# Plain gathers for the whole first fill, two sets of transposes moved to round 12, and row indices for the joint table

## What is computed

```python
V = emb_v[x]                                   # 32 fields x 2048 x 64
iu, ju = np.triu_indices(F, k=1)               # 496 pairs
VV = V[iu] * V[ju]
hid = jax.nn.relu(jnp.einsum('pbk,kh->pbh', VV, at_w) + at_b)
score = jnp.einsum('pbh,ho->pbo', hid, at_h)
pooled = jnp.sum(VV * score, axis=0)
logit = pooled @ p + w0 + jnp.sum(w1[x], axis=0)
prob = jax.nn.sigmoid(logit)
```

## Time and profile before

| | |
|---|---|
| median of 3 runs | 843.81 us (842.17 to 844.33) |
| the profiled execution | 845.1 us, its span 843.2 us |
| PE (TensorE matmul) busy | 784.8 us, 93% |
| DVE (VectorE) busy | 721.6 us, 86% |
| ACT (ScalarE) busy | 640.4 us, 76% |
| POOL (GpSimd) busy | 538.4 us, 64% |
| share of DMA engines taken by the gathers' queue | 45.3% |
| granted TensorE clock, mean | 0.98 |

### The profile page before, as it was taken

One profiled execution on the slowest core, in us unless ns is written; L12 is line 12 of the kernel. 1 busy time (PEld: TensorE's weight loads), 2 busy tenths in 40 slices (PEclk: granted clock), 3 DMA queues, 4 the chain that ended last, 5 costly groups with the idle time before them and its releaser, 6 DMA issues.

```text
span 843.2 us, 26432 instructions
## 1 busy us (share of the span) xinstructions
PE 784.8 (93%) x10550; PEld 278.6 (33%) x10550; DVE 721.6 (86%) x1221; ACT 640.4 (76%) x676; POOL 538.4 (64%) x529
## 2 busy tenths in 40 slices
PE   0467699999999999999999999999999999999998
PEld 0123233333333333333333333333333333333332
DVE  2456678999999999999999999999999999999894
ACT  0255477888888888888888888888888888888785
POOL 4377566667767666677676666776766667767600
PEclk9869799999999999999999999999999999999999
DMA  8589625444334446543243456833445546633300
GB/s 190 157 25 25 25 21 24 21 22 24 21 21 24 22 21 22 22 24 22 20 24 23 21 22 22 24 22 20 23 22 22 22 22 23 23 21 23 12 0 2
DMA packets 19135, 24.17 MB, mean 29 GB/s; under 512 B 9704, under 2 KB 9773, under 8 KB 19117
## 3 DMA queue, kind: packets, MB, share of 16 engines
q0 software_dynamic: 16640, 17.07, 45.3%
q1 hardware_dynamic: 1535, 6.64, 2.1%
q10 hardware_dynamic: 942, 0.22, 0.1%
HBM read 20.59 MB, written 3.31 MB: 28 GB/s over the span
## 4 chain that ended last, share of the span: by engine, by line
PE 88%; POOL 4%; DMA 4%; issue 2%; ACTq 1%; DVE 0%; SPq 0%; ACT 0%; POOLq 0%
PE Z L574 53%; PE SG L590 27%; POOL rows L287 4%; PE SG L604 4%; PE Z L538 4%; DMA rows<-table,joint_idx 2%; DMA tail_w<-in_L_rec_w_dram 1%; DMA table<-tail 1%; DVE joined L344 0%; PE Z L666 0%; ACTq L476 0%; ACTq L477 0%; ACTq L478 0%; ACTq L473 0%; PE Z L647 0%
## 5 line engine op out<-in xcount | busy, mean ns | idle before, releaser
L287 POOL DMA_INDIRECT rows<-table,joint_idx x504 | 521.5, 1035 | 251.4 <-issue 146.5
L431 DVE TENSOR_TENSOR X<-V 128x992 f32<-128x992 f32 (+15 forms) x1024 | 634.8, 691 | 31.8 <-ACT V L487 18.4
L513 ACT ACTIVATE H<-Z,bias 128x1024 f32<-128x1024 f32 x512 | 528.9, 1120 | 114.3 <-PE Z L574 110.8
L574 PE MATMUL Z<-X,w_sb 64*64 64x512 f32 x4096 | 478.0, 602 | 6.8 <-DVE X L431 3.2
L574 PEld LDWEIGHTS Z<-X,w_sb 64*64 64x64 f32 x4096 | 147.3, 133 | 288.9 <-issue 282.7
L590 PE MATMUL SG<-H,score_w 128*32 128x512 f32 x2048 | 239.4, 597 | 0.0
L590 PEld LDWEIGHTS SG<-H,score_w 128*32 128x32 f32 x2048 | 56.8, 109 | 172.8 <-issue 96.2
L457 ACT ACTIVATE pV<-V,pmask 128x1024 f32<-128x1024 f32 x64 | 81.6, 1277 | 0.1
L399 DVE TENSOR_TENSOR prod<-SG,gram 128x512 f32<-128x512 f32 x32 | 22.1, 692 | 65.4 <-PE SG L590 65.4
L446 ACT COPY V<-Z 128x1024 f32<-128x1024 f32 x31 | 31.4, 1012 | 43.4 <-PE Z L538 43.4
L604 PEld LDWEIGHTS SG<-V,pV 128*32 128x32 f32 x4096 | 43.4, 110 | 21.9 <-issue 19.9
(11 more groups left out here) (46 smaller groups left out, 38.6 us busy)
## 6 DMA issues: line engine op xcount, KB each, us to landing
rows<-table,joint_idx POOLq DMA_INDIRECT x504, 3.8
table<-joined SPq DMA_DIRECT2D x4, 792.0 KB
H<-in_L_rec_emb_v_dram SPq DMA_DIRECT2D x4, 768.0 KB, 10.2
idx_raw<-in_r_x_dram SPq DMA_DIRECT2D x2, 64.0 KB, 2.0
idx_raw<-in_r_x_dram ACTq DMA_DIRECT2D x2, 64.0 KB, 2.2
rows<-in_L_rec_emb_v_dram,idx POOLq DMA_INDIRECT x8, 7.9
w_all<-in_L_rec_w_dram,idx POOLq DMA_INDIRECT x8
table<-tail SPq DMA_DIRECT2D x1, 54.7 KB
```

The source lines that it names most:

```text
L287: pool.indirect_dma_start(out=rows[t % 2][:, g * FILL_M + m, half, c0:c1], out_offset=None, in_=source, in_offset=bass.IndirectOffsetOnAxi ...
L431: last_one = nc.vector.tensor_tensor(xo, vj, vi.unsqueeze(3).to_broadcast(shape), ALU.mult)
L513: nc.scalar.activation(H[:, s % H_SLOTS, :, COLS * g:COLS * g + COLS], Z[:, z_slot(r), :, :], ACT.Relu, bias=bias[:, 0:1]).then_inc(hid_re ...
L574: done = nc.tensor.matmul(Z[64 * par:64 * par + 64, z_slot(r), half, :], w_sb[k, :], X[k, s % X_SLOTS, par, COLS * g:COLS * g + COLS], sta ...
```

## The change

Three things are changed.

1. All 16 gathers of fill 0 are plain, so only fill 1 waits for the joint table. The w1 values of fill 0 then all come from single-value gathers at the end, 16 instead of 8, and `keep_w1(0, 0)` is dropped. The counts of `w1_kept` and `w1_first` follow.
2. In fills 1 and 2 the transposes of the next fill (the third and the fourth one) stand before round 12 instead of round 6. ScalarE's `keep_v` moves with them, and its pV halves and w1 copies from relus 12 and 14 to 14 and 15. Slots and waits follow. As these two fills now differ from the rest, they are straight code on every engine, and the loop begins with fill 3.
3. A joint gather takes `table` as rows of 66 values with the row index `idx` and a constant offset of `half` values. `joint_idx` and the two VectorE operations that made it are dropped.

```diff
-TURN_BEFORE = 6
+TURN_BEFORE, LATE_TURN = 6, 12
+LATE_FILLS = (1, 2)
...
+JOINT_AT = (0, 1)
+PLAIN_FILLS = 1
...
+def turn_before(t):
+
+    return LATE_TURN if isinstance(t, int) and t in LATE_FILLS else TURN_BEFORE
...
-    return (r if r < TURN_BEFORE else r + 1) % Z_SLOTS
+    return (r if r < turn_before(t) else r + 1) % Z_SLOTS
...
-    return r - 2 if TURN_BEFORE <= r < TURN_BEFORE + 2 else r - 3
+    return r - 2 if turn_before(t) <= r < turn_before(t) + 2 else r - 3
...
             fill(0, 0, True, False)
-            with eng.Fori(1, FILLS - 2, 2) as t:
+            fill(1, 1, False, False)
+            fill(2, 0, False, False)
+            with eng.Fori(3, FILLS - 2, 2) as t:
...
-                for g in groups:
-                    joint = t > 0 or g > 0
-                    source, at_rows = (flat, joint_idx) if joint else (emb_v, idx)
+                joint = t >= PLAIN_FILLS
+                for g in range(2):
...
-                                                    in_=source,
-                                                    in_offset=bass.IndirectOffsetOnAxis(ap=at_rows[:, col:col + 1], axis=0)
+                                                    in_=table if joint else emb_v, element_offset=JOINT_AT[half] if joint else 0,
+                                                    in_offset=bass.IndirectOffsetOnAxis(ap=idx[:, col:col + 1], axis=0)
...
-            plain_w1 = [(2 * half, n) for half in range(2) for n in range(FILL_M)]
+            plain_w1 = [(Q, n) for n in range(PLAIN_FILLS * FILL_M) for Q in range(QUARTERS)]
...
-            gather(0, groups=(0,))
-            pool.wait_ge(idx_ready, 4)
+            gather(0)
+            pool.wait_ge(idx_ready, 2)
             pool.wait_ge(table_stored, 16 * (PIECES + 1))
-            gather(0, groups=(1,))
             gather(1)
             pool.wait_ge(first_turned, 2)
-            pool.wait_ge(w1_kept, 2)
             gather(2)
             for t in range(3, FILLS):
                 pool.wait_ge(rows_turned, t - 2)
-                pool.wait_ge(w1_kept, 2 * (t - 1))
+                pool.wait_ge(w1_kept, 2 * (t - 1 - PLAIN_FILLS))
                 gather(t, paced=True)
...
-            dve.wait_ge(idx_ready, 2)
-            for half in range(2):
-                cols = slice(half * 2 * NM, (half + 1) * 2 * NM)
-                nc.vector.tensor_scalar(joint_idx[:, cols], idx[:, cols], float(JOINT), float(half), ALU.mult, ALU.add
-                                        ).then_inc(idx_ready, 1)
...
-                        if r == TURN_BEFORE:
+                        late = turn_before(t) == LATE_TURN
+                        if r == turn_before(t):
                             keep_v(t + 1, 1 - parity)
-                        if r == 12:
+                        if r == (14 if late else 12):
                             keep_pv(t + 1, 1 - parity, 0)
                             keep_w1(t + 1, 1 - parity)
-                        if r == 14:
+                        if r == (15 if late else 14):
                             keep_pv(t + 1, 1 - parity, 1)
...
-                        keep_w1(0, 0)
...
-                if r == TURN_BEFORE + 2 and not first and not last:
+                if r == turn_before(t) + 2 and not first and not last:
...
-                    if r == TURN_BEFORE and not first and not last:
-                        pe.wait_ge(hid_ready, ROUNDS * t + TURN_BEFORE - Z_SLOTS + 1)
+                    if r == turn_before(t) and not first and not last:
+                        pe.wait_ge(hid_ready, ROUNDS * t + turn_before(t) - Z_SLOTS + 1)
                         turn(t + 1, 1 - parity)
...
             products(0, 0, True, False)
-            products(1, 1, False, False, head)
-            with pe.Fori(1, FILLS - 2, 2) as t:
+            products(1, 1, False, False)
+            products(2, 0, False, False)
+            products(3, 1, False, False, head)
+            with pe.Fori(3, FILLS - 2, 2) as t:
```

23 lines of the change are left out of this document (10 added, 13 removed).

## The result

| | before | after |
|---|---|---|
| median of 14 runs each | 843.55 us (842.17 to 844.90) | 847.30 us (842.40 to 850.32) |
| ratio, 95% interval | | 1.0040 (1.0026 to 1.0054) |
| the profiled execution | 845.1 us, span 843.2 | 850.3 us, span 848.0 |
| PE busy | 784.8 us | 789.7 us |

The changed kernel is 0.4% slower. The forecast was 830.4 us and a range of 822.5 to 839, so it was wrong in sign and in size. The runs of the changed kernel spread over 7.9 us, those of before over 2.7; the profiled one is its slowest, so its trace shows the loss at its largest.

What follows compares the result with a forecast made beforehand. The prediction took TensorE to bound the steady fills and a line of GpSimd and DMA gathers the head; 19.7 - 1.8 - 4.5 = 13.4 us gained, so 831.7 profiled and 830.4 us median, range 822.5 to 839.

Steps and rivals of the forecast that it cites:

- S: Delay of the joint table from eight more plain gathers beside its stores: 2.5 us taken, between 0.7 and 4.2, extreme 12.3.
- the prediction's own line: Landing time of joint gathers before the change: 34.2 us + 1.54 us x number, counted from the first one.
- Part 1: Head: eight joint gathers less before fill 1, so its transposes come at 61.4 us, ruled by landing.
- The 19.7 us at round 12: Fill 1: rounds 6 to 11 fill the wait for rows, so round 12 starts at 87.3 us instead of 107.02.
- F: Theory made after the result: TensorE's instruction blocks wait behind gathers' packets; gaps need new straight code and full DMA engines.
- The 1.8 us back in fill 3: The gap where the loop begins moves to fill 3, with no wait to lie under: 1.8 us lost.
- The late pV, 0.7 twice: Two late fills: ScalarE's pV is done 8.1 us after the transposes' start, PE wants it at 7.4; 1.4 us lost.
- Fills 3 and 4, E = 4.5 us: Fill 4's transposes wait 3.1 us for rows, fill 3's even; with 1.4 for pV, 4.5 us lost (1.4 to 8.5).
- Edits of no price: Row-wise index, eight more w1 gathers at the end and dropped fill 0 w1 copies were claimed to cost nothing.
- the rival of a longer gather: GpSimd: row-wise index with constant lengthens each joint gather; at 1.56 us, 25 us lost, giving 855; chance 0.05.
- (b): Rival at the head: table stores starved by gathers, 12.3 us late, round 12 at 97.1, giving 840.2; chance 0.12.
- (d): Rival: fetching two more straight fills while DMA engines are at 0.90 eats the 13.4 us gain, giving 843.8; chance 0.07.

Runs made afterwards that it cites:

- thin gathers: The changed kernel with every gather of fills 1 to 31 fetching one value for each partition instead of 65: 829.4 us, 0.9868 of the kernel before.
- copies: The changed kernel with gathers of fills 1 to 31 replaced by tiny transfers, plus sixty 512 KB copies on SP's queue: 852.9 us, 1.0148 of the kernel before.
- the parts alone: Kernel before with only the plain gathers and row index: 1.0141, 1.0103; with only late transposes and straight fills 1 and 2: 1.0010, 1.0013, 1.0008 of it.

## Why the prediction was wrong

**The size of S, the cost on the table.** This is the first step that failed: 2.5 us forecast, from bytes at 363 GB/s (0.7) and engine time in a light window (4.2), and 11.1 measured. The prediction's own sign of being wrong, a first joint gather after 40 us, came true at 44.19. The end called the extreme, 12.3, was the nearest. The reasoning by bytes fell: beside gathers the engines move half as much (169 to 187 GB/s). The row that said so was on hand, the first eight gathers' landing at 22.53 us beside the loads, and was put under a rival. The Trainium skill, "DMA: Bandwidth & Descriptors", section "Queues, rings and completion order", has the engines go round their queues packet by packet, and it spoke against the change. The trace agrees in so far as both queues are served in the same 15 us, the gathers' with 55.5% of the engines' time and the stores' with 39.0%; single turns it doesn't show. With 11.1 in the prediction's own line, fill 1 comes at 70.0; it came at 70.92. So eight plain gathers cost 11.1 us and save eight joint ones, 12.3: Part 1 moves work of nearly the same price from one side of the table to the other: 1.2 us by this sum, 0.3 us as measured (71.17 to 70.92). Fill 0's second group was off by the same cause: forecast between 28 and 34.8 us, it came at 38.69, which cost nothing, as fill 1's rows came later still.

**The 19.7 us at round 12.** The mechanism held: the work of rounds 6 to 11 filled the wait, no wait was left before fill 2's transposes. The gain was 10.2. Of the 9.5 us missing, 8.6 are S. In the rest is the step "that place is now straight code, so 14.5": the gap is still there with 1.48 us, in straight code. It was never the loop's entry: the row of before has it behind the 14th matmul, two ahead of the place where the loop begins. It ends 1.3 to 1.6 us after a packet of q8 in both profiles, and it is 0 with thin gathers and 2.52 with copies, so it is a wait for a block of instructions. This misreading mattered more than its size, since the gap was the one sight of F in the trace of before.

**The 1.8 us back in fill 3.** No gap of its own there; fill 3's first rounds took 1.5 us more at the lower clock, after the gaps.

**The late pV, 0.7 twice.** Fill 2's grams waited 0.44 us; fill 3's lie among the gaps, where no wait for pV can be seen. The 0.21 us at fill 1's grams isn't part of it: their order is as before, where they waited 0.83. Mechanism right, size somewhat smaller.

**Fills 3 and 4, E = 4.5 us.** No wait for rows at all: both had room. In this place stand the gaps, 9.1 us, which no term of the sum had, with some 2.5 us of matmuls at the lower clock between them, 1.5 in fill 3's first rounds, and 0.9 of short pauses in fill 4's. This is the second step that failed, and the one that turned a gain into a loss: that the filled pause costs only waits for rows, 4.5 us. The prediction saw that GpSimd's pause would go and the queue stay full, and asked only who waits for rows.

**Edits of no price.** The row index: GpSimd's mean joint gather is 1040 ns for 1035, so the rival of a longer gather is out.

```profile
L293 POOL DMA_INDIRECT rows<-table,idx x496 | 515.7, 1040 | 249.6 <-issue 144.2
```

The w1 gathers: nothing here, some 12 us on the chips of 1134 us.

**The rivals.** (b), stores starved, had round 12 9.9 us earlier, and it came 10.2 us earlier: it describes the head. From that gain it took 1.8 and 4.5 us and came to 840.2. What was lost instead in the profile after is 9.1 us of gaps, 0.4 us at the pV and some 5 us of slower or paused matmuls, 15 us, so that its span is 4.8 us longer; this execution is the slowest of 14, and the median lost 3.75 us. The gaps are (d)'s mechanism, with a chance of 0.07: fetching straight code while the engines are full. Its size was off too: not one price for each new piece of code, but a block that comes some 13 us late and the one behind it. Why this block and not those from 88 to 107 us, with the engines at 0.85 to 0.88 as well, isn't shown. The two rivals were priced as alternatives, 0.12 and 0.07, but they add. What the chances lacked is the case of both. That they are tied, because a later table and a filled pause keep the queue full when the new code is wanted, is argued and not shown.

## To carry to other kernels

A DMA that is issued earlier isn't free because the engine that issues it was idle: count what the DMA engines are doing then, and price a gather of 128 rows by the slope of its landings under load (1.54 us here; 11.1 us for eight), not by its bytes. When a pause in a long queue of gathers is filled, look for what used the pause: here TensorE's next instructions. When a gap in the middle of a row of matmuls stands at the same place in two kernels and has no releaser, look for a packet of instructions just ahead of its end. If there is one, try the unrolled code where the DMA engines have room; no run here did that with a gain.

## What the runs showed of the hardware

A block of 16 KB of TensorE's instructions came some 13 us late behind gathers, though such blocks take 0.1% of the DMA engines' time in all. Beside gathers at a share of 0.85 to 0.92 TensorE stood 5.1 and 4.0 us, and beside copies from SP's queue (1.22, with packets that overlap) 3.1 and 2.5, each time until a block had come. A full queue isn't enough by itself, as blocks also came in even steps beside a share of 0.85 to 0.88. And chips differ, or what goes on beside them: on four, the kernel before takes 1109 to 1138 us instead of 843, and on one of these the changed kernel takes 833 us without the gathers, as fast as on the others. What makes the gathers so costly there stays open; late blocks it isn't, as the loop fetches none. Open is also which part of the change brings the gaps on a chip of 843 us, since the parts alone met only the others.
